# Four groups of edges move from the mixer to the channel product of a two-layer graph network

## What is computed

```python
xn = _layernorm(x, axis=-1)
# graph part: messages of 50000 edges, sorted by destination, added up at their destinations
agg_h = segment_sum((feat * norm_out)[src], dst, num_segments=N)
agg_e = segment_sum(edge_feat, dst, num_segments=N)
rst = concatenate([agg_h, agg_e], axis=1) @ weight
# mixer part: 256 -> 768 channels, batch norm over all nodes, relu, attention per node
h = conv1d(h, w_qkv, pad=2)
h = batchnorm(h, bn_gamma, bn_beta)
h = relu(h)
...
out = einsum('ngde,ngdl->ngdl', vk, q) / (sum(v, -1, keepdims=True) + ATT_EPS)
ft = conv1d(ft, w_res, pad=0) + b_res
x = x + gnn(xn) + mix(xn)
```

## Time and profile before

| | us |
|---|---|
| median of 3 runs | 2156.36 |
| lowest and highest of them | 2155.73 to 2157.47 |
| the profiled execution | 2150.83 |
| its span in the trace | 2148.8 |

### The profile page before, as it was taken

How to read it: one execution, slowest core, us unless ns; L and a number is a source line. 1 busy time by engine, 2 the same in 40 slices (tenths; PEclk the granted TensorE clock), 3 DMA queues, 4 the chain that set the end, 5 groups by cost and what they waited for, 6 DMA issues and landing times. The chain is left out here.

```text
span 2148.8 us, 35685 instructions
## 1 busy us (share of the span) xinstructions
PE 1792.6 (83%) x10583; PEld 1407.2 (65%) x10584; DVE 1246.1 (58%) x3264; ACT 708.2 (33%) x1624; POOL 992.5 (46%) x1571
## 2 busy tenths in 40 slices
PE   7499689885667999999965999879999763999976
PEld 5266466663536999999952556547777641988865
DVE  6654796996555444444458658834554665333436
ACT  4222344544420212121217931133222230333334
POOL 0676886884201222222220547888885000455542
PEclk9999899998886999999987999979999885999988
DMA  7565654553740111111123324444443237122234
GB/s 240 152 156 136 161 151 117 157 154 90 297 179 20 33 33 34 33 33 34 31 84 102 108 62 159 119 128 118 141 130 99 85 126 294 56 66 62 65 82 132
DMA packets 171241, 239.50 MB, mean 111 GB/s; under 512 B 74145, under 2 KB 139261, under 8 KB 168692
## 3 DMA queue, kind: packets, MB, share of 16 engines
q0 software_dynamic: 42336, 112.74, 18.4%
q1 hardware_dynamic: 116884, 113.45, 16.1%
q10 hardware_dynamic: 11904, 11.96, 1.8%
HBM read 184.86 MB, written 56.12 MB: 112 GB/s over the span
## 5 line engine op out<-in xcount | busy, mean ns | idle before, releaser
L658 POOL DMA_INDIRECT agg_message<-table,edges_src x638 | 631.5, 990 | 118.0 <-issue 95.2
L2827 PEld LDWEIGHTS ex_p_h<-ex_xT,ex_own_up 128*128 128x128 f32 (+1 forms) x2464 | 281.2, 192 | 2.7 <-issue 1.4
L2827 PE MATMUL ex_p_h<-ex_xT,ex_own_up 128*128 128x128 f32 (+1 forms) x2464 | 282.0, 276 | 1.0 <-DVE ex_xT L2878 1.0
L2786 POOL DMA_INDIRECT ex_x<-moe_in,route_token_at x58 | 57.3, 987 | 311.6 <-PE ex_p_x L2817 242.2
L2882 DVE COPY ex_own_up<-moe_up 128x1280 f32 x114 | 100.5, 882 | 168.7 <-PE ex_p_h L2827 167.9
L657 POOL MEMSET agg_rest<- 128x1 f32 x638 | 79.9, 125 | 202.8 <-DMA table<-layer_XN 75.0
L2952 POOL DMA_INDIRECT ex_x<-moe_in,route_token_at x66 | 64.3, 975 | 173.9 <-PE ex_p_x L2983 90.7
L2870 ACT ACTIVATE ex_gate_h<-ex_p_h 128x640 f32<-128x640 f32 x56 | 39.4, 704 | 315.2 <-PE ex_p_h L2827 315.2
L3023 ACT COPY ex_own_up<-moe_up 128x1024 f32 x66 | 68.9, 1046 | 209.8 <-PE ex_p_h L2996 169.3
L2996 PEld LDWEIGHTS ex_p_h<-ex_xT,ex_own_up 128*128 128x128 f32 x1024 | 119.3, 195 | 16.4 <-issue 15.0
L717 PE MATMUL agg_partial<-agg_message,moe_up 128*64 128x321 f32 x638 | 108.9, 479 | 24.6 <-issue 10.5
(11 more groups left out here) (666 smaller groups left out, 3692.9 us busy)
## 6 DMA issues: line engine op xcount, KB each, us to landing
moe_up<-in_f_w SPq DMA_DIRECT2D x8, 1386.0 KB, 20.2
agg_message<-in_edge_rows SPq DMA_DIRECT2D x54, 192.0 KB
agg_message<-table,edges_src POOLq DMA_INDIRECT x638
sums<-agg_span SPq DMA_DIRECT2D x107, 80.2 KB
moe_up<-in_f_w SPq DMA_DIRECT2D x4, 2048.0 KB, 14.7
moe_down<-in_f_w SPq DMA_DIRECT2D x4, 2048.0 KB
sums<-agg_span SPq DMA_DIRECT2D x107, 64.0 KB
moe0b_down<-in_f_w SPq DMA_DIRECT2D x8, 768.0 KB
```

The costliest lines, as they stand in the source:

```text
L658: pool.indirect_dma_start(out=to[:, k * w:k * w + D], out_offset=None, in_=self.table, in_offset=bass.IndirectOffsetOnAxis(ap=self.edges.s ...
L2827: return pe.matmul(to, own_up[:, o:o + n], xT[:, k * D + c * P:k * D + (c + 1) * P], start=(c == 0), stop=(c == 1))
```

## The change

One number changes:

```diff
-QKV_GROUPS = 15
+QKV_GROUPS = 19
```

## The result

| us | before | after |
|---|---|---|
| median (7 runs each, same chip) | 2155.73 | 2162.07 |
| lowest and highest | 2151.00 to 2157.47 | 2158.91 to 2164.52 |
| the profiled execution | 2150.83 | 2159.92 |
| its span | 2148.8 | 2157.8 |

The changed kernel is slower: ratio 1.0036, 95% interval 1.0026 to 1.0045. The forecast was 2163.5. The two traces differ by 9.0 us, the medians by 6.3.

A forecast was written before the change was run, and what follows sets the result against it. GpSimd's gathers were taken to end the first block and VectorE to pace the mixer. +15.0 - 2.0 - 1.1 - 4.8 = +7.1 us on a median of 2156.4 gave 2163.5, range 2158.5 to 2169.5.

The forecast's parts named there:

- GpSimd ends the first block: Channel product: GpSimd's last gather ends at 243.5, 9 us behind TensorE, so gathers set the block's end.
- Rival A: Channel product: TensorE, not GpSimd, ends the block; term 9.7, sum +1.8, time 2158.2; chance 0.14.
- The block's term: Channel product: four groups' gathers cost 30.0 us less 15.0 of waiting, +15.0; bounds 12.6 to 17.
- The loss under L997: End of the channel product: a gather beside VectorE's long product loses 2.35 us again; 2.2 to 3.5 by the skill's rule.
- TensorE: +12.2 for +9.7: Channel product: four groups' products at 2.42 us each add 9.7 us to TensorE, hidden by GpSimd's later end.
- The mixer's start, nothing added: Mixer's start: same work in the same order moves as a whole, nothing added; bound 1.5 us for a lower clock.
- Marks -2.0: Mixer, VectorE: 31 marks instead of 34 between first tile and last tile's product, 0.66 us each, -2.0 us.
- the late interval -1.1: Mixer's last interval: gathers no longer fall behind, so 10.86 becomes 9.80, -1.1 us.
- The tail, -4.8: Mixer's end: last turning follows the product at once; saves 6.0 at full clock, 3.6 at lower clock, middle -4.8 us.
- rival C: Mixer gives less back: tail stays and start is colder; +12 to +14.5, 2169.5; chance 0.14.
- rival D: Channel product: dealt-out order makes TensorE wait a few us, hidden by GpSimd; forecast's time, chance 0.63 together with the forecast.

The follow-up runs named there:

- e1: The changed kernel with GpSimd gathering two groups ahead over the block boundary instead of three; 2154.61, ratio 1.0004 to the kernel before.
- e8: The kernel before with L997, the scaling of the head's counts, moved from the channel product's end to the mixer's start; 2152.40, ratio 0.9988.
- f1: The kernel before (15 groups) with groups 51 to 53 behind the last tile's residual product and L997 moved to the mixer's start; 2144.58, ratio 0.9956.
- f4: The kernel before with 17 groups, groups 51 to 53 behind the last residual product, L997 moved to the mixer's start, gathers two ahead; 2147.40, ratio 0.9974.
- f3: The changed kernel (19 groups) with groups 51 to 53 behind the last tile's residual product; 2159.25, ratio 1.0026 to the kernel before.
- e7: The changed kernel with L997, the scaling of the head's counts, moved to the mixer's start; 2157.93, ratio 1.0013 to the kernel before.

## Why the prediction was right, point by point

**GpSimd ends the first block: right.** Its last gather ends 10.3 us behind TensorE's last product, and e1 takes the loss away by moving gathers alone. Wrong was a side step: "GpSimd ends it already, 4 us behind TensorE". I compared the last busy rows of engines. The block ends when the last store has landed, 3.3 us behind TensorE's last product, so the true lead was 1.5 us (from e8, f1 and f4), and L997 lay between. Rival A would have given 8.2 for the block, not 9.7. For the change itself it made no difference.

**The block's term: +18.5 for +15.0, above its bound of 17.** From the gathers' and memsets' grouped rows (busy 102.1 + 13.1, gaps 17.8 + 15.0 before):

```profile
L658 POOL DMA_INDIRECT agg_message<-table,edges_src x126 | 126.4, 1003 | 23.2 <-issue 18.3 <-POOL agg_rest L657 3.5 <-POOLq L936 0.2
L657 POOL MEMSET agg_rest<- 128x1 f32 x126 | 15.7, 125 | 0.5 <-PE agg_partial L721 0.5
```

126 gathers for 102: 24.3 us more of gathers, 2.6 of memsets and 5.4 of gaps, together 32.3, less 14.5 of waiting, and 0.7 because the block itself began later in this execution. Against my terms: the loss under L997 was 3.25 and not 2.35, which I had carried over (+0.9; the gather now began with L997 and not 1.0 behind it); 24 gathers cost 31.4 without that and not 30.0, 1.31 each (+1.4); the wait gave 0.5 less; the later beginning of the block was 0.7. The loss lies within the 2.2 to 3.5 that the prediction worked out for a gather held by L997, and the held gather began 10 us ahead of the block's end, so it isn't a matter of being the last. I had taken the gather's price from one undisturbed group, and the mean of many is dearer: a gather issued just behind the start of a mark takes 1.23, as this pair of the kernel before shows. That marks make up the whole 1.4 isn't shown.

```profile
223.53 0.54 DVE L695 TENSOR_TENSOR moe_up<-edges_node,edges_rel 128x384 f32<-128x384 f32 x1
223.65 1.23 POOL L658 DMA_INDIRECT agg_message<-table,edges_src  x1 [0.19 <-issue]
```

**TensorE: +12.2 for +9.7.** Its first steps are 1.75 later already at step 2 (0.7 the block's later beginning, the rest slower first products and a longer wait for edge features); the rest is 10.4 for four groups. Hidden, as said.

**The mixer's start, nothing added: right.** The first reciprocal comes 20.4 us behind the start in both.

**Marks -2.0 and the late interval -1.1: right.** The rhythm kept 9.14 and 9.80, and no interval of 10.86 is left at the end. Between first and last reciprocal it is 251.1 for 256.1, 5.0 less. What I hadn't seen is 1.7 of it: VectorE's stall on the head's counts.

```profile
355.20 0.69 DVE L1181 TENSOR_TENSOR mix_prod<-mix_cat,layer_XN 128x512 f32<-128x512 f32 x1 [11.84 <-ACT mix_square L1263]
```

It was 13.51 in the kernel before, and goes from 8.6 to 13.6 over these kernels. The dealt order, which sets the groups around the head's products, is not all of it: e1 has the changed kernel's order and 13.51, with TensorE at a lower granted clock there. So this 1.7 is not a gain that the change brings for certain.

**The tail, -4.8: the measured -4.2 lies between the two ends given.** The mechanism was right, and the condition named (the lower clock in the residual product) came true, though the turning stayed at 0.63. The 1.9 us for that product at the lower clock stood on no row of its own; it measured 1.69 (3.68 for 1.99), and 1.79 in f3. The 4.8 was the middle between two outcomes, and the clock fell between the two steps, so that the middle came near is luck. That is half of rival C; its other half, a colder start of the mixer, didn't come. Of rival D nothing is seen: TensorE's delay in the first block is that of its products and its first steps.

**The sum.** +18.5 - 5.0 - 4.2 and 0.1 elsewhere is +9.4 at the mixer's end, +9.0 in the span, for +7.1 forecast. Term by term that is +3.5 for the block, -1.9 for VectorE's stretch, +0.6 for the tail, 0.1 elsewhere, and -0.3 behind the mixer: the profiled execution was due at 2157.9 and took 2159.9. The step from there to the median missed by -3.4: I had added the 5.5 us that the kernel before's profile lay under its median, and the changed kernel's lies 2.2 under. So 2163.5 was near 2162.07 by luck in part, since terms that missed by +2.0 in all met a difference of runs that missed by -3.4. What the traces do show is which engine ends the block, and that the mixer gives back less than the block loses. Why executions of the kernel before spread over 6 to 9 us one trace can't show.

## What to carry to other kernels

When work moves between blocks, price every resource that it carries by itself: here TensorE had the higher share and GpSimd's gathers decided, so the products could move and the gathers stay. Where a block ends for all engines at once, add to each engine's last row what hangs behind it (a copy, a store's landing) before calling one of them the last, since a gain reaches only to the next of these chains. The last chain of a loop is worth a look of its own: taking three groups out from in front of the last turnings brought 0.4%, as much as the whole loss under study, and moved nothing between the blocks. It did so in the kernel with late gathers alone; with 19 groups the same edit brought about 0.1%, and the last chain got longer. And before two traces are compared to less than a microsecond or two, the block's own beginning has to be looked at: here it hid 1.4 us of a gain of 2.1.

## What the runs showed of the hardware

- An indirect gather of 128 rows issued under a VectorE product of two SBUF inputs lasted until 0.8 us behind that product's end (3.30 and 4.20 for 0.95). Where the product is moved (e7, e8), the block's last gathers take 0.95 again and one at its new place takes 3.10. Issued 0.1 us behind the start of a mark's short product (0.55 us) a gather took 1.23.
- The stretch from TensorE's last sum to the next block, over ACT's copy and SP's store, is 3.28 us; from GpSimd's last gather it is 0.81 to 0.83.
- TensorE's granted clock was 0.62 in a residual product behind 4 us with 1.24 of work, and the product took 3.68 us; it was 1.00, and 1.99 us, where the pause before was 1.0. Behind a pause of 6.46 us the turning took 1.09 and the product 3.78, at 0.50.
